# VectorE makes the low part of the attention output between those of q and k: a linear-attention and MoE kernel on one core

## The reference

```python
qkv = layernorm(x) @ w_qkv                       # 4096 x 768
q, k = elu(rope(q) * SCALE) + 1, elu(rope(k) * SCALE) + 1
kv, ks = kv + k_t v_t, ks + k_t                  # a scan over the tokens
out_t = (q_t kv) / max(q_t ks, 1e-6)
x = x + out @ w_out
y = layernorm(x)
h_e = silu(y @ Wg[e]) * (y @ Wu[e])              # 8 experts of inner width 256
x = x + sum_e weights[e] * (h_e @ Wd[e])
```

## Time and profile before

| | |
|---|---|
| time, median of 3 runs | 798.66 us (795.63 to 800.37) |
| time of the profiled execution | 795.7 us |
| its span (first to last instruction) | 793.7 us |
| mean granted TensorE clock | 0.993 of full speed |
| busy: PE / PEld | 770.3 us (97%) / 667.3 us (84%) |
| busy: DVE / ACT / POOL | 606.7 (76%) / 465.6 (59%) / 483.3 us (61%) |
| chain that ended last | PE 85%, DVE 6%, POOL 2%, DMA 2%, ACT 2% |

### The profile page before, as it was taken

One profiled execution on the slowest core, in us unless ns is written; L12 is line 12 of the kernel. 1 busy time (PEld: TensorE's weight loads), 2 busy tenths in 40 slices (PEclk: granted clock), 3 DMA queues, 4 the chain that ended last, 5 costly groups with the idle time before them and its releaser, 6 DMA issues.

```text
span 793.7 us, 18504 instructions
## 1 busy us (share of the span) xinstructions
PE 770.3 (97%) x6882; PEld 667.3 (84%) x6882; DVE 606.7 (76%) x1597; ACT 465.6 (59%) x886; POOL 483.3 (61%) x537
## 2 busy tenths in 40 slices
PE   8877899999999999999999999999999999999998
PEld 8766688888888888888888888888888888888887
DVE  6798888878777797779877797778887788756344
ACT  3665767666666656666666566656656665644222
POOL 3795778755566576655666665565676656653322
PEclk9999999999999999999999999999999999999999
DMA  4555214122111121222101221120311121100000
GB/s 143 129 120 98 69 54 93 41 44 69 41 41 23 22 67 41 42 43 58 39 15 40 43 68 41 41 43 14 56 42 41 41 55 28 28 2 28 1 1 27
DMA packets 97321, 38.30 MB, mean 48 GB/s; under 512 B 74192, under 2 KB 96976, under 8 KB 97232
## 3 DMA queue, kind: packets, MB, share of 16 engines
q1 hardware_dynamic: 90704, 30.83, 18.2%
q10 hardware_dynamic: 6528, 6.29, 2.7%
HBM read 16.13 MB, written 4.19 MB: 26 GB/s over the span
## 4 chain that ended last, share of the span: by engine, by line
PE 85%; DVE 6%; POOL 2%; DMA 2%; issue 2%; ACT 2%; SPq 1%; DVEq 0%; ACTq 0%; POOLq 0%
PE y L486 22%; PE gate L452 21%; PE up L452 21%; PE front L312 5%; PE back L364 3%; PE back L408 3%; PE front L313 2%; PE up L383 2%; PE up L420 1%; POOL a_lo L1199 1%; PE front L335 1%; PE back L352 1%; PE back L395 1%; PE front L433 1%; PE back L335 1%
## 5 line engine op out<-in xcount | busy, mean ns | idle before, releaser
L1228 POOL TENSOR_TENSOR h_lo<-work,h_hi 128x512 fp32r<-128x512 f32 x126 | 163.2, 1295 | 59.2 <-ACT h_hi L688 59.2
L1199 POOL TENSOR_TENSOR a_lo<-am,a_hi 128x512 f16<-128x512 f32 x120 | 145.0, 1210 | 53.9 <-ACT a_hi L615 51.4
L486 PE MATMUL y<-wd_hi,h_hi 128*128 128x256 f32 x504 | 145.8, 289 | 0.0
L486 PE MATMUL y<-wd_lo,h_hi 128*128 128x256 f32 x504 | 140.4, 279 | 0.0
L486 PE MATMUL y<-wd_hi,h_lo 128*128 128x256 f32 x504 | 140.2, 278 | 0.0
L1072 DVE TENSOR_TENSOR work<-work,up 128x512 f32<-128x512 f32 x128 | 87.0, 679 | 61.7 <-PE up L452 61.4
L688 ACT ACTIVATE h_hi<-work 128x512 fp32r<-128x512 f32 x126 | 79.4, 630 | 58.2 <-DVE work L1072 36.4
L1088 DVE SCALAR_TENSOR_TENSOR xa<-y,wo,xa 128x256 f32<-128x256 f32 x252 | 111.9, 470 | 1.9 <-PE y L486 1.9
L486 PEld LDWEIGHTS y<-wd_hi,h_hi 128*128 128x128 f32 x504 | 94.7, 188 | 4.1
L486 PEld LDWEIGHTS y<-wd_lo,h_hi 128*128 128x128 f32 x504 | 94.9, 188 | 2.8
L615 ACT ACTIVATE a_hi<-am 128x512 f16<-128x512 f32 x120 | 74.8, 624 | 35.4 <-DVE am L850 35.4
(11 more groups left out here) (228 smaller groups left out, 1774.3 us busy)
## 6 DMA issues: line engine op xcount, KB each, us to landing
xr<-xT SPq DMA_DIRECT2D x32, 128.0 KB, 2.4
xa<-x SPq DMA_DIRECT2D x32, 128.0 KB, 2.6
out<-xa SPq DMA_DIRECT2D x32, 128.0 KB, 1.7
xa<-Wg ACTq DMA_DIRECT2D x8, 256.0 KB, 2.8
work<-Wd ACTq DMA_DIRECT2D x8, 256.0 KB, 3.1
work<-Wu ACTq DMA_DIRECT2D x8, 256.0 KB, 2.9
work<-w_qkv SPq DMA_DIRECT2D x2, 384.0 KB, 3.8
qT<-q_st SPq DMA_TRANSPOSE x32, 3.2
```

The source lines that it names most:

```text
L486: m = pe.matmul(y_bank(n, t), h_at(hi, n)[:, t * P:(t + 1) * P], wd_p[wi][:, u // KI, u % KI, :], start=(n % KI == 0 and (t % 2 == 0 or n ...
L1199: pool.tensor_tensor(a_p[1][:, heads(r), :], am_place(g, r).rearrange("p (h n) -> p h n", h=4), a_p[0][:, heads(r), :], ALU.subtract).then ...
L1228: pool.tensor_tensor(h_at(1, n), hb[:, n % 2, :], h_at(0, n).bitcast(F32), ALU.subtract).then_inc(s_hlo, 1)
```

## The change

In the loop, VectorE runs `o_lo(c)` between `q_lo(a)` and `k_lo(a)`. Before, it ran behind both. Nothing else is edited; the head and the tail, and the lists of the other engines, are as before.

```diff
-                route_first(router); norm(c); route_second(router); q_lo(a); k_lo(a); o_lo(c); h_up(n + 1)
+                route_first(router); norm(c); route_second(router); q_lo(a); o_lo(c); k_lo(a); h_up(n + 1)
```

## The result

| | before | with the change |
|---|---|---|
| time, median of 6 runs each | 796.07 us (795.45 to 800.37) | 804.49 us (803.72 to 807.65) |
| profiled execution: time / span | 795.7 / 793.7 us | 804.16 / 802.3 us |
| mean granted TensorE clock | 0.993 | 0.995 |
| busy: PE / DVE / ACT | 770.3 / 606.7 / 465.6 us | 775.0 / 605.7 / 465.5 us |

The ratio is 1.0099, 95% interval [1.0078, 1.0119]: the change makes the kernel about 1% slower, 8.4 us by the medians and 8.6 by the spans.

The account below looks back on a forecast made before the run. TensorE, never idle in the steady loop, was taken to bound the kernel. 27 x 0.33 = 8.9 us gave 804.6 on the profiled execution, 807.6 on the median; the forecast between them was 806.5 us, range 801 to 811.

Parts of the forecast that it names:

- What bounds the kernel: In the steady loop TensorE has matmuls in flight for 40.00 of 40 us; other engines cost only by making it wait.
- When `o_lo` can start: On VectorE, `o_lo` must wait for ScalarE's `o_hi`, so it starts only 0.17 us earlier than before.
- What it gives to proj: proj's weight load can start at 416.15 instead of 416.32, regaining most of the exposed 0.07 us per step.
- What it does to `h_up` and `up`: `h_up` starts 0.43 us later, `up`'s load at 417.35 instead of 417.01; TensorE loses 0.33 us per step.
- The exposure that was read from a gate's wait: Behind a late weight load, the next matmul pair starts 0.57 us after the load, read where a gate waited for silu.
- Does it come back?: Claimed that TensorE has no idle time left to give, so the lost time per step is not regained.
- The one case in the trace of before: One step where VectorE waited 1.60 instead of 1.24 us before `q_lo`; it took 22.90, and 0.39 was not recovered.
- What else is late: Later `silu` leaves the gate's load 0.11 us, about 0.05 needed; `x1_add` isn't late; k's transpose stays hidden: no cost.
- second wait: Rival: the load of `gate(n + 3)` is also late behind `silu(n + 2)`, 3.0 us more, 809.5 us; chance 0.09.
- that cover: The 1.4 us between k's transpose landing and being wanted; were it gone, each 0.1 would cost 2.7 us.
- The clock: TensorE's clock stays full despite the gaps; rival: `up` behind each gap runs at 1.2 GHz, 37 us more, chance 0.02.
- The sum: Over the loop, 27 steps of 0.33 us lost on TensorE make 8.9 us, +1.1%.

Follow-up runs that it names:

- kernel 2: Against the kernel before, VectorE's `o_lo` moved last, behind `h_up`: order `q_lo`, `k_lo`, `h_up`, `o_lo`; 816.81 us, ratio 1.0256.
- kernel 5: The change, with ScalarE's `o_hi(c)` moved ahead of `v1(a)`; 806.7 us beside 797.68 of the kernel before, ratio 1.0111.
- kernel 6: The change, with one more VectorE instruction, its result unused, between `o_lo` and `k_lo`; 814.8 us beside 796.57 of the kernel before, ratio 1.0234.
- kernel 1: The change, with `h_up(n + 1)` moved ahead of `k_lo(a)`; 796.64 us beside 795.91 of the kernel before, ratio 1.0011.
- kernel 3: The change, with `h_up(n + 1)` moved ahead of `q_lo(a)`; 802.02 us beside 795.91 of the kernel before, ratio 1.0080.
- kernel 4: The kernel before, with `h_up(n + 1)` moved ahead of `q_lo(a)`; 803.20 us beside 795.91 of the kernel before, ratio 1.0091.

## Why the prediction was right

**What bounds the kernel: right.** TensorE had no idle time, and each lateness at this place came out in the plain step's length, one for one (kernels 2, 5, 6).

**When `o_lo` can start: right.** 1.03 behind `q_lo` for 1.04. `o_hi` sets it, and `o_hi` itself hangs on `o_T`: moved ahead on ScalarE it gained only 0.04.

**What it gives to proj: right in kind and size.** The exposed load went; its worth, 0.07 per step, shows only where `h_up` is out of the way (22.46 or 22.44 against 22.52).

**What it does to `h_up` and `up`: right, the step that decides.** `h_up` 0.43 later as worked out, the load of `up` 0.32 later for 0.34, TensorE's loss 0.33 per step. The exposure that was read from a gate's wait fits: load to second pair is 422.19 - 421.61 = 0.58, for 0.57.

**"Does it come back?": right.** The one case in the trace of before pointed the right way, though the 22.90 from `q_lo` to `q_lo` is VectorE's own lateness; what TensorE lost shows in the `st_add` interval that begins in step 18, 22.87 against 22.52. `k_hi` was not what held `q_lo` there: it had ended at 391.67, 0.46 ahead, where 0.10 is usual. What did is open. But the price followed the lateness in every kernel. Against step 19, `o_lo` and `h_up` were 0.35 late before, and 0.35 was lost; in the change, where `o_lo` hangs on `o_hi`, they were 0.24 late, and 0.20 was lost; in kernel 5 `q_lo` was as late but `o_lo` not at all, and 0.03 was lost.

**What else is late: right.** `silu(n + 2)` ended at 422.77 and the gate's load started at 422.89, 0.12 to spare for 0.11; no second wait appeared. `x1_add` followed `h_up` with no wait. k's transpose was hidden. In the first interval that cover was thin, as kernel 1 showed, but the change's smaller delay didn't reach it (23.87, 0.35 above before, like any other).

**The clock: right.** The granted clock was 1.00 in the first step, which had the larger gaps, and 1.00 through the loop (88 to 705 us), so that the 0.995 of the whole comes from the head (0.83 from 60 to 80 us); the swing that the Trainium skill ("TensorE: Matmul & The Clock Gate", A second HAM failure mode) describes did not occur.

**The sum.** 8.9 us foretold, 8.48 measured in the loop: 26 intervals of 0.33, and the gap of step 31 (0.29) falls behind the last `st_add` counted. The absolute time was 2.0 too high, since the median of the first three runs of before (798.66) was itself above that of six (796.07); the profiled execution's 795.7 + 8.9 = 804.6 would have met the 804.49.

## What to carry to other kernels

On an in-order engine, ask what stands behind a wait, not what stands at it. `k_lo` had been filling the time in which `o_hi` was made; taken out of there, it ran afterwards, in front of `h_up`, which had less than 0.1 us to spare. When an instruction is pulled ahead, put behind its wait only work that nobody is waiting for: `o_lo, h_up, k_lo` has the same wait and gains 0.06 us in a plain step.

Where the bound engine is full, take the slack of each wait from the trace (end of the releasing row to start of the waiting one, less what a release needs); beyond it, lateness was paid in full here, step by step. And check special steps apart: the orders that were best in plain steps lost in router steps and in the loop's first.

## What the runs showed of the hardware that was not expected

Two of VectorE's small router instructions (L1027 and L1029) stand still while GpSimd runs `h_lo`. L1027 (128 x 32) took 0.66 us before, where it started inside an `h_lo`, and ended with it; in the change it started as one was about to end and took 0.19. The kernel before, and then the change:

```profile
370.67 1.30 POOL L1228 TENSOR_TENSOR h_lo<-work,h_hi 128x512 fp32r<-128x512 f32 x1
371.37 0.66 DVE L1027 TENSOR_TENSOR router<-router,q_m 128x32 f32<-128x32 f32 x1
```
```profile
374.43 1.29 POOL L1228 TENSOR_TENSOR h_lo<-work,h_hi 128x512 fp32r<-128x512 f32 x1
375.58 0.19 DVE L1027 TENSOR_TENSOR router<-router,q_m 128x32 f32<-128x32 f32 x1
```

370.67 + 1.30 = 371.97, and L1027 ends at 372.03. In the change L1027 starts at 375.58, as `h_lo` is about to end at 375.72. In all kernels each of the two that took over 0.25 us ended 0.04 to 0.06 us behind an `h_lo`. The large VectorE instructions of the same stretch, which read one operand from PSUM (`k_lo` and `h_up`), keep their 0.68 us beside `h_lo`, and so does a small reduction (L1036, 0.17 us). This agrees with the Trainium skill ("SBUF — State Buffer", Who interferes with whom): a VectorE instruction with two SBUF inputs contends with a GpSimd instruction that reads SBUF, and the port pair that they share is an exclusive lock. That it is this that cost kernels 2 to 5 their time behind router steps rests on the rows' ends; it wasn't tried apart.

In the four steps of the first expert batch, the load of `up` followed `h_up` by 0.10 to 0.12 us instead of 0.05. There it also waits for the weights' low parts; that the second wait is the reason was not tested.
